# One third of an expert's weight split, moved ahead of the Silu and of the gating product, in a macaron block of mixture of experts, latent attention and mixture of experts

## The reference

```python
x = x + 0.5 * ffn(layernorm(x))
x = x + attn(layernorm(x))
x = x + 0.5 * ffn(layernorm(x))

def ffn(x):                       # 8 experts, 2 of them for each token
    logits = x @ gate                             # 256 -> 8
    w, idx = top_k(logits, 2); w = softmax(w)
    combine = sum over k of w[k] * one_hot(idx[k], 8)
    h0 = x @ w0[e]; h1 = x @ w1[e]                # 256 -> 512, each expert
    return sum over e of combine[e] * ((silu(h0) * h1) @ wo[e])   # 512 -> 256
```

## Time and profile before

| | |
|---|---|
| Median of 3 runs | 1191.51 us (1191.1 to 1193.56) |
| The profiled execution | 1193.56 us, span 1191.7 us |
| Mean granted clock of PE | 0.957 of full speed |
| Busy, share of the span | PE 88%, PEld 73%, DVE 69%, ACT 52%, POOL 42% |
| First expert stage | from about 84 to 290 us of the span |
| Second expert stage | from about 981 us to the end |

### The profile page before, as it was taken

One profiled execution on the slowest core, in us unless ns is written; L12 is line 12 of the kernel. 1 busy time (PEld: TensorE's weight loads), 2 busy tenths in 40 slices (PEclk: granted clock), 3 DMA queues, 4 the chain that ended last, 5 costly groups with the idle time before them and its releaser, 6 DMA issues.

```text
span 1191.7 us, 24657 instructions
## 1 busy us (share of the span) xinstructions
PE 1043.2 (88%) x6200; PEld 867.2 (73%) x6201; DVE 824.7 (69%) x1750; ACT 616.5 (52%) x1340; POOL 502.7 (42%) x464
## 2 busy tenths in 40 slices
PE   4579999995646999999999999999989729999995
PEld 4557888784634888888888888888778627887884
DVE  5365556643765999999999999999835455565552
ACT  1243334321125888888888888888810123343321
POOL 2542333333223555555555566655412532333332
PEclk9999999998677999999999999999999859999998
DMA  9844445332100011111010110011464463454231
GB/s 238 248 163 98 99 105 137 61 55 48 36 1 1 10 36 37 35 35 35 35 35 35 35 35 28 27 34 35 142 218 146 129 221 98 106 143 111 44 52 15
DMA packets 71562, 95.41 MB, mean 80 GB/s; under 512 B 9600, under 2 KB 48640, under 8 KB 71296
## 3 DMA queue, kind: packets, MB, share of 16 engines
q1 hardware_dynamic: 57216, 78.04, 21.3%
q0 software_dynamic: 14304, 16.87, 7.8%
HBM read 64.37 MB, written 34.43 MB: 83 GB/s over the span
## 4 chain that ended last, share of the span: by engine, by line
PE 47%; DMA 26%; issue 11%; DVE 4%; POOL 4%; ACT 1%; POOLq 1%; SPq 0%; DVEq 0%; ACTq 0%
DMA out<-shared,small 12%; DMA x_after_moe<-shared,small 12%; PE bank L1535 9%; PE bank L1551 7%; PE bank L1525 6%; PE bank L1552 5%; PE bank L1526 5%; PE bank L1527 5%; PE bank L1514 2%; POOL rows_by_expert L529 2%; PE bank L1515 2%; PE bank L1616 1%; PE bank L1476 1%; PE bank L1352 1%; PE bank L1354 1%
## 5 line engine op out<-in xcount | busy, mean ns | idle before, releaser
L810 ACT ACTIVATE shared<-bank,small 128x512 f32<-128x512 f32 x256 | 175.8, 687 | 57.9 <-DVE small L1184 55.5
L1184 DVE TENSOR_REDUCE small<-bank 128x1 f32<-128x512 f32 x256 | 175.2, 685 | 37.8 <-PE bank L1527 27.6
L1214 DVE TENSOR_TENSOR split_rows_and_inner<-bank,shared_split 128x512 fp32r<-128x512 f32 x256 | 174.7, 682 | 7.0 <-ACT shared_split L819 5.0
L762 ACT CAST split_rows_and_inner<-bank 128x512 fp32r<-128x512 f32 x78 | 45.7, 586 | 246.7 <-PE bank L1337 246.7
L1535 PE MATMUL bank<-constants,shared 128*128 128x128 f32 x1024 | 155.2, 274 | 0.9 <-ACT shared L810 0.9
L1551 PE MATMUL bank<-shared_split 128*128 128x256 f32 x512 | 144.4, 304 | 5.5 <-DVE shared L1208 2.2
L819 ACT CAST shared_split<-bank 128x512 fp32r<-128x512 f32 x256 | 147.3, 575 | 1.0 <-PE bank L1535 1.0
L1354 PE MATMUL bank<-expert_weights_low,split_rows_and_inner 128*128 x312 | 144.1, 462 | 0.0
L1356 PE MATMUL bank<-expert_weights_high,split_rows_and_inner 128*128 x312 | 143.0, 458 | 0.0
L1551 PEld LDWEIGHTS bank<-shared_split 128*128 128x128 f32 x512 | 96.3, 188 | 56.4 <-issue 27.3
L1552 PE MATMUL bank<-split_rows_and_inner,shared_split 128*128 128x256 f32 x512 | 132.8, 282 | 0.0
(11 more groups left out here) (191 smaller groups left out, 2483.8 us busy)
## 6 DMA issues: line engine op xcount, KB each, us to landing
expert_weights<-L_ffn_w_kernel SPq DMA_DIRECT2D x32, 512.0 KB, 4.6
shared<-rows_by_expert SPq DMA_DIRECT2D x78, 129.0 KB, 2.1
expert_weights<-L_ffn_wo_kernel SPq DMA_DIRECT2D x16, 512.0 KB, 6.1
shared<-inverse_sums SPq DMA_DIRECT2D x64, 128.0 KB, 2.9
attended_transposed<-shared SPq DMA_DIRECT2D x32, 256.0 KB, 2.7
expert_weights<-attended_transposed SPq DMA_DIRECT2D x2, 2048.0 KB, 10.2
shared<-attended_transposed SPq DMA_DIRECT2D x2, 2048.0 KB, 10.6
rows_by_expert<-empty_rows SPq DMA_DIRECT2D x23, 129.0 KB, 3.5
```

What stands on the lines that cost most here:

```text
L810: nc.scalar.activation(prob[k % 2], bank[k % 4][:, :], ACT.Exp, bias=negmax[:, k % 8:k % 8 + 1], accum_out=psum[par][:, k % 8:k % 8 + 1]). ...
L1184: V.tensor_reduce(negmax[:, k % 8:k % 8 + 1], bank[k % 4][:, :], AX.X, ALU.max, negate=True).then_inc(max_ready, 1)
L1214: V.tensor_tensor(pTl[k // 2 % 2][:, :, at], bank[4 + k % 2][:, :].rearrange("p (c n) -> p c n", c=GT), pTh[k // 2 % 2][:, :, at].bitcast( ...
```

## The change

In a tile that has a split, ACT now makes the high part of piece 0 between `it_high(t-1)` and the Silu, and the wait for the loaded weights moves with it. DVE makes the low part of piece 0 between `xt_low(t+1)` and the product of Silu and h1. Pieces 1 and 2 stay where they were. ACT and DVE have one branch more in each tile but the first.

```diff
@@ scalar engine, step(i, k) @@
                         it_high(t - 1)
+                        with act.If(e > 0):
+                            act.wait_ge(w_in[f], e * 48 + 48)
+                            split_high(f, e, 0)
                     act.wait_ge(h0_psum[f], t + 1)
                     nc.scalar.activation(gated, bank[4][:, :], ACT.Silu).then_inc(silu_ready[f], 1)
                     if not is_last(i, k):
                         xt_high(t + 1, (k + 1) % 3)
                     if not is_first(i, k):
                         with act.If(e > 0):
-                            act.wait_ge(w_in[f], e * 48 + 48)
-                            split_high(f, e, 0)
                             split_high(f, e, 1)
                             act.wait_ge(y_psum[f], t)
                             split_high(f, e, 2)
@@ vector engine, step(i, k) @@
                     if not is_last(i, k):
                         xt_low(t + 1, (k + 1) % 3)
+                    if not is_first(i, k):
+                        with dve.If(e > 0):
+                            split_low(f, e, 0)
                     multiply(t)
                     keep_tag(t, i, k)
                     if not is_first(i, k):
-                        with dve.If(e > 0):
-                            split_low(f, e, 0)
                         scale(t - 1, (k - 1) % 3)
                         with dve.If(e > 0):
                             split_low(f, e, 1)
```

## The result

The changed kernel takes 1203.07 us (median of 4, 1202.18 to 1204.48) against 1192.53 us of the kernel before (median of 4, 1191.1 to 1193.82). The ratio is 1.009 with a 95% interval of 1.0073 to 1.0107: 0.9% slower, 10.5 us by the medians. Predicted were 1201.5 us and +10.0 us.

The account below looks back on a forecast made before the run. Two paces, PE's and that of the queued adds, were taken to bound the expert stages. Six split tiles a stage at 0.93 us, less 0.47 and 0.70 covered, gave +10.0 us on 1191.5: 1201.5 us, range 1195.5 to 1209.5.

Parts of the forecast that it names:

- a new wait of PE: In each split tile, ahead of the transposes: PE stands still 1.56 us for DVE's late multiplication.
- the old wait: PE's 0.93 us stall ahead of the outer product, waiting for DVE's it_low; only 0.30 us of it left.
- the tile's price: Each of 12 split tiles gets 0.93 us longer, as it_low on DVE comes that much late.
- What the adds cover: At the stages' ends the queue of adds hides 0.47 us of PE's slowdown in stage one and 0.70 in two.
- Tiles without a split: The added branches on ACT and DVE cost 0 there, with 0.1 us for 66 tiles as upper bound.
- in the other direction nothing is gained: At the stages' ends, a faster PE gains nothing beyond 0, as long as the adds keep their pace.
- Both stalls adding: Rival: in split tiles PE's new and old stalls stand one behind the other, 1.56 us a tile, 1209.0 us; chance 0.12.
- The adds hiding it: Rival: the queue of adds in the expert stages hides the loss, no change, 1191.5 us; chance 0.09.
- Faster: Rival: ACT's cast fills idle time, it_low is on time and PE's stall goes, about 1185 us; chance 0.07.
- Transfers that collide more: Rival: a change in how transfers collide makes it slower by more; chance 0.03.
- The clock: Rival: the new stall brings PE to 1.2 GHz for the tile after, 59 us more, about 1260; chance 0.02.

Follow-up runs that it names:

- ACT's half: Only the cast of piece 0 moved ahead of the Silu on ACT, DVE's order as in the kernel before: 1213.80 us, ratio 1.0069 to before.
- ACT's half doubled: Casts of pieces 0 and 1 ahead of the Silu on ACT, DVE as in the kernel before: 1212.96 us, ratio 1.0147 to before.
- the first series: First timing of the changed kernel against the kernel before: 1203.07 us, ratio 1.009.
- the second: The changed kernel timed once more, unchanged, beside a kernel before of 1205.01 us: 1214.40 us, ratio 1.0074.
- run 2: Not a run label: words of "they run 2 us a stage faster", said of the adds with piece 2's low part put off, 2.03 and 1.99 us shorter.
- the put-off piece: DVE's low part of piece 2 put off to the next tile, from the kernel before: 1187.02 us, ratio 0.996.
- the adds unchained: Adds go in turn to three tensors, two thirds of sums left out: from the kernel before 1190.93 us, ratio 0.9987; with the change 1200.20 us, 1.0066.
- the doubled change: Pieces 0 and 1 both moved ahead of the Silu and of the multiplication, against the kernel before: 1254.24 us, ratio 1.0415.
- DVE's half doubled: Low parts of pieces 0 and 1 ahead of the multiplication on DVE, ACT as in the kernel before: 1219.86 us, ratio 1.0213.

## Why the prediction was right

**The mechanism held.** The Silu behind one cast, xt_low behind the Silu, multiplication about 2.1 us late (2.06: 123.27 - 119.98 against 113.51 - 112.28), a new wait of PE ahead of the transposes, the old one partly inside it. Of the figures that I gave for the trace, the new wait is 1.49 us where 1.56 stood. The rest of the old wait is 0.57 us where I had said about 0.3, so less of it is covered than I had worked out. Over a split tile and the next one, 1.8 us above two quiet tiles is right only when it is counted from where the Silu would have started: from the cast's start at 119.85 to the Silu at 131.40 it is 11.55 us, 1.78 above two tiles of 4.88 or 4.89. From Silu to Silu, as my sentence reads, it is 131.40 - 120.80 = 10.60, only 0.83 above.

**The size** of the tile's price was 0.93 and is 0.87: (5.19 + 5.22) / 12. The cast puts the Silu off by 0.95 and not 1.06 us, since I had divided a row of three by three, and xt_low by 0.94; in return the step from xt_low to split_low is 0.44 and not 0.33. These two nearly cancel. The 0.06 us that is left lies between the multiplication and the two later splits: 124.33 - 123.27 = 1.06 us, where I had added up 0.72 + 0.40. That DVE's unbroken work sets the price, and not the new wait of PE, is shown by ACT's half: a wait of 0.24 in place of 1.49 and nine tenths of the loss. It is confirmed by that half doubled, 1.73 us a tile where 1.75 was computed in the same way.

**What the adds cover** was read right: 0.47 and 0.70 us were predicted from the tails, and the stages give 5.19 - 4.71 = 0.48 and 5.22 - 4.53 = 0.69. The stages' adds together are 9.24 us longer, the whole kernel 10.5 us in the first series and 9.4 (1214.40 - 1205.01) in the second. So the 10.0 of my sum should be held against 9.24: it was 0.8 too high, and that it lies so near the 10.5 of the first series is in part luck, as 1.3 us of the 10.5 are not in the stages.

**Tiles without a split** pay nothing, as assumed: scaling follows scaling in about 4.9 us in both profiles.

**One sentence was wrong though it changed nothing in the sum:** that in the other direction nothing is gained. It rested on the adds keeping their pace, and with PE's stalls gone they run 2 us a stage faster. It is the time to the landings that is shorter (the waits for them 2.9 and 1.9 us less). Why, stays open: the put-off piece leaves the order of all transfers as it was, and may only shift when they meet, which no run here singles out.

**The rivals.** Both stalls adding: no, only 0.57 of 1.08 was left, and the price is 0.87, not 1.56. The adds hiding it: no, the queue ran empty. Faster: no. Transfers that collide more: nothing points to it, as with the adds unchained the stages lengthen by nearly the same (5.1 us each). The clock: not in this change, granted 1.00 in both stages with waits of 1.5 us. It falls only in the doubled ones: in 11 of 12 split tiles of the doubled change, and in 4 of 12 with DVE's half doubled. Beside it stood a rule of the Trainium skill, TensorE: Matmul & The Clock Gate, "A second HAM failure mode: psum-queue depth-cycling", by which frequent micro-idles between groups of matmuls make the clock swing. The runs here don't bear it out in that form: three shorter waits in a tile (ACT's half doubled) left the clock at 1.00, and what brought it down were waits of 2.4 us alone and of 2.65 us behind one of 0.85. Had the change moved two pieces, a sum without the clock would have been some 18 us too low (49 against the 31 expected).

## What to carry to other kernels

- Work that has time is not moved ahead of work that hasn't on an in-order engine because that engine idles somewhere: ask what stands behind the insertion up to the next value that TensorE needs, on that engine and on the next. Here the moved cast of 1.05 us cost 0.79 us by itself, and 0.87 together with its subtraction, six times a stage.
- Where a queue and an engine are nearly equally long, read the lag at the stage's end against the lag of an item that found no queue. The difference is how much later the engine may finish for nothing; read as 0.47 and 0.70 us, it came out as 0.48 and 0.69. What removing a stall gives can't be read so; that needs the run in which both limits go.
- Price a stall twice, at full clock and with a fall behind it, when single waits of TensorE go from 1.5 towards 2.5 us.

## What the runs showed of the hardware

- TensorE's granted clock held at 1.00 behind single waits of 1.5 us (changed kernel) and behind three shorter ones of 2.8 us together (ACT's half doubled), fell in 4 of 12 tiles behind a wait of 2.4 us (DVE's half doubled) and in 11 of 12 behind 0.85 and 2.65 us close together (two pieces ahead). A fall cost about 1.5 us a time (13.65 against 12.16 us, and 14.79 against 13.22), and up to 2.7 in the three tiles in which the clock stayed at 0.50 for about 6.8 us instead of 3.4 (intervals of 7.63 to 7.73 instead of 4.99).
- The kernel before took 1192 to 1194 us in three series and 1205 us in one, at nearly the same lengths inside the expert stages: the scalings of the changed kernel are 194.97 us long with chained adds in the group of 1205, and 194.92 with unchained ones in that of 1192. Between these two profiles 9 us of the surplus lie ahead of the first scaling (104.01 against 95.06) and 3.4 us between the stages. Each group ran on another chip; whether the chip makes the difference no run here shows.
- An add into the result lands later when an expert's weights are being loaded beside it: in the unchained kernel five adds of the first stage took 7.3 to 7.8 us from issue to landing, most of the others 3.6 to 3.9.
